# Second attention: the order of two VectorE steps, the low half of the transposed weights and the row maximum, within a half slot

## What is computed

```python
x = x + _L1_attn_ref(_layernorm(x, axis=-1), ...)

Q1, Q2 = (Q[..., :dh], Q[..., dh:])
K1, K2 = (K[..., :dh], K[..., dh:])
lam = (lam1 - lam2 + LAMBDA_INIT)[None, :, None, None]
A1 = jnp.einsum('bhqd,bhkd->bhqk', Q1, K1) * scaling
A2 = jnp.einsum('bhqd,bhkd->bhqk', Q2, K2) * scaling
attn = jax.nn.softmax(A1, axis=-1) - lam * jax.nn.softmax(A2, axis=-1)
O = jnp.einsum('bhqk,bhkd->bhqd', attn, V)
rms = jnp.sqrt(jnp.mean(O * O, axis=-1, keepdims=True) + EPS)
O = O / rms * rms_scale
O = O * (1.0 - LAMBDA_INIT)
return jnp.einsum('bne,de->bnd', O, Wo)
```

## Time and profile before

| | us |
|---|---|
| median of three runs (2936.09 to 2948.23) | 2939.1 |
| the profiled execution | 2946.47 |
| its span, first to last instruction | 2944.7 |
| PE busy in the span | 2752.8 (93%) |
| DVE busy | 2317.6 (79%) |
| ACT busy | 2126.2 (72%) |
| POOL busy | 1801.3 (61%) |

### The profile page before, as it was taken

One profiled execution on the slowest core, in us unless ns is written; L12 is line 12 of the kernel. 1 busy time (PEld: TensorE's weight loads), 2 busy tenths in 40 slices (PEclk: granted clock), 3 DMA queues, 4 the chain that ended last, 5 costly groups with the idle time before them and its releaser, 6 DMA issues.

```text
span 2944.7 us, 46590 instructions
## 1 busy us (share of the span) xinstructions
PE 2752.8 (93%) x16447; PEld 2032.8 (69%) x16447; DVE 2317.6 (79%) x4143; ACT 2126.2 (72%) x4692; POOL 1801.3 (61%) x1357
## 2 busy tenths in 40 slices
PE   6999999999899999999999999999999999999996
PEld 3333333333347777788888888888888888888885
DVE  8888888888937877789788777777777778777876
ACT  2677777777766555677877777777777787777773
POOL 3442524332015555677788777788778787777773
PEclk8899999999989999999999999999999999999997
DMA  1000000000022111000000000000000000000000
GB/s 41 7 7 7 12 7 7 7 7 2 2 76 75 48 48 58 8 1 1 1 1 3 3 1 3 3 1 3 3 1 3 3 1 3 3 1 3 3 3 6
DMA packets 25689, 34.83 MB, mean 12 GB/s; under 512 B 4136, under 2 KB 14952, under 8 KB 25456
## 3 DMA queue, kind: packets, MB, share of 16 engines
q1 hardware_dynamic: 25456, 31.85, 3.4%
HBM read 29.08 MB, written 2.23 MB: 11 GB/s over the span
## 4 chain that ended last, share of the span: by engine, by line
PE 67%; DVE 15%; ACT 8%; issue 6%; POOL 5%; DMA 0%; DVEq 0%; POOLq 0%; ACTq 0%
PE P L1798 18%; PE P L1666 9%; PE P L1825 8%; PE P L1809 6%; PE P L1651 5%; PE P L1727 5%; PE P L1639 4%; ACT a_PT L784 4%; DVE c_nm L1376 4%; DVE c_DT L1401 3%; PE P L1781 3%; PE P L1738 2%; PE P L1835 2%; PE P L1629 2%; POOL d_tn L1099 2%
## 5 line engine op out<-in xcount | busy, mean ns | idle before, releaser
L1376 DVE TENSOR_REDUCE c_nm<-P 128x1 f32<-128x1024 f32 x512 | 624.4, 1220 | 303.9 <-PE P L1798 301.9
L908 ACT ACTIVATE c_P<-P,c_nm 128x1024 f32<-128x1024 f32 x512 | 573.0, 1119 | 251.8 <-DVE c_nm L1376 247.5
L1221 DVE TENSOR_REDUCE a_mx<-P 128x1 f32<-128x512 f32 x1024 | 640.2, 683 | 99.5 <-PE P L1639 95.4
L784 ACT ACTIVATE a_PT<-P 128x512 f32<-128x512 f32 x1024 | 537.1, 603 | 165.4 <-PE P L1651 165.2
L2048 POOL TENSOR_TENSOR c_P<-c_P,c_P 128x1024 f32<-128x1024 f32 (+1 forms) x256 | 623.0, 2434 | 21.3
L2046 POOL TENSOR_SCALAR c_P<-c_P,c_rr 128x1024 f32<-128x1024 f32 (+1 forms) x256 | 300.9, 1176 | 338.4 <-DVE c_rr L1388 338.4
L1825 PE MATMUL P<-c_DT,c_xkh 128*128 128x256 f32 x2048 | 451.7, 283 | 24.7 <-DVE c_Yl L1409 23.0
L1651 PE MATMUL P<-a_Qs,a_Ks 32*128 32x512 f32 x1024 | 344.2, 493 | 59.6 <-ACT a_PT L784 53.2
L1825 PEld LDWEIGHTS P<-c_DT,c_xkh 128*128 128x128 f32 x2048 | 350.2, 189 | 37.0 <-DVE c_Yl L1409 29.2
L1798 PE MATMUL P<-c_xth,c_Th 128*128 128x512 f32 x1024 | 365.1, 437 | 2.8 <-ACT c_P L908 2.8
L1401 DVE TENSOR_TENSOR c_DT<-P,c_DT 128x512 fp32r<-128x512 f32 x512 | 348.4, 681 | 9.0 <-ACT c_DT L919 8.8
(11 more groups left out here) (245 smaller groups left out, 5393.6 us busy)
## 6 DMA issues: line engine op xcount, KB each, us to landing
b_cwB<-cw_scratch SPq DMA_DIRECT2D x64, 256.0 KB, 5.0
c_stg<-in_cw SPq DMA_DIRECT2D x8, 640.0 KB, 4.0
a_Qs<-a_mT SPq DMA_DIRECT2D x256, 2.0 KB
b_stg<-in_moe SPq DMA_DIRECT2D x9, 384.0 KB, 3.0
out<-xres SPq DMA_DIRECT2D x15, 128.0 KB, 1.8
xres<-in_x SPq DMA_DIRECT2D x3, 512.0 KB, 7.6
xres<-in_x SPq DMA_DIRECT2D x2, 256.0 KB, 3.0
a_hTl_f<-in_wqk SPq DMA_DIRECT2D x1, 512.0 KB, 3.6
```

The lines of the kernel that those rows point to most:

```text
L784: e.activation(m.PT[j][hs % 4][:, :], bank("scores", u, hs, j), ACT.Exp, scale=SCALE).then_inc(m.S["a_exp"])
L908: e.activation(m.P1[s][n % 4][:, :], P[:, k:k + 2, :].rearrange("p c k -> p (c k)"), ACT.Exp, bias=m.nm[:, n % 4, s:s + 1], accum_out=m.sm ...
L1221: e.tensor_reduce(m.mx2[u % 2][:, t // 4, j, t % 4, half:half + 1], bank("maxima", u, t, j, half), AX, ALU.max).then_inc(m.S["a_max_dve"])
L1376: e.tensor_reduce(m.nm[:, n % 4, s:s + 1], P[:, k:k + 2, :].rearrange("p c k -> p (c k)"), AX, ALU.max, negate=True).then_inc(m.S["c_nm"])
```

## The change

The step `low` is taken from behind `score` (and behind what was left of the experts) and put right behind `turn`, ahead of `score`:

```diff
@@ -473,13 +473,12 @@
         for s in range(2):
             if 3 <= n < NTAU + 3:
                 on_ring("turn", n - 3, s)
+                p.do("low", n - 3, s)
             if n < NTAU:
                 p.on(slots.take(), "score", n, s)
             left = next(moe_left, None)
             if left is not None:
                 experts(left)
-            if 3 <= n < NTAU + 3:
-                p.do("low", n - 3, s)
             if s == 0 and 0 < n <= NTAU:
                 p.do("combine", n - 1)
```

## The result

The changed kernel takes 3196.5 us (median of 4 runs, 3189.1 to 3207.5) against 2943.7 us of the kernel before (4 runs with the later one): 1.085 times as long, 95% interval 1.083 to 1.088. The difference of the medians is +252.8 us; the forecast was +253, at 3193.

The account below looks back on a forecast made before the run. TensorE set the pace at 3.31 us a half; after the change a ring through VectorE and ScalarE would: 1803 + 85 + 5 + 31 = 1924 us against 1671.5, +253, so 3193 us, range 3150 to 3250.

Parts of the forecast that it names:

- The ring's links: Second attention: exponential to copy 1.10, copy to low half 0.61, low half to maximum 0.60, maximum to exponential 1.26 us.
- the ring: Second attention: ScalarE's exponential and copy, VectorE's low half and maximum wait on each other in turn, once per half; 1803 us.
- Work in the ring: ScalarE's steps between exponential and copy: weigh 70, fourth layer's normalisation 12, layernorm's high halves 3 us; together +85 us.
- the bare ring: A half of the second attention with nothing between exponential and copy takes 3.57 us, against 3.31 before.
- Work beside the ring: ScalarE's steps between copy and exponential, +5 us, and VectorE's steps behind the maximum, +31 us, where they exceed the room.
- the term of VectorE: VectorE's steps behind the maximum, some of them the fourth layer's, exceed the room in 55 halves: +31 us.
- the third rival: TensorE's clock falls in part of the second attention, 232 us more in a fifth of the halves: 3425 us; 4%.
- the clock: TensorE in the second attention, busy for 83% at a clock near 1; costed at nothing.
- One sign: In the profile after, TensorE would wait for the exponential to free the scores' banks; its 35.3 us for low halves would go.
- The first rival: The low half fills VectorE's gap before the maximum as intended, kernel not slower: 2904 us; 3%.
- The second rival: The maximum is pushed back only where ScalarE's copy ends late, 320 copies by 165 us: about 3104 us; 4%.

Follow-up runs that it names:

- the first experiment: The changed kernel with ScalarE's weigh put behind the copy of the next half instead of ahead of it: 3126.2 us.
- the fourth experiment: Transposes and ScalarE's copy put ahead of the exponential of the half before: in the changed kernel 2896.8 us, in the kernel before 2947.9 us.
- the second experiment: The changed kernel with the low half ahead of the maximum only in halves s = 1: 2953.0 us; only in s = 0: 2998.7 us.
- experiments 5 and 6: 5: changed kernel, low half of the half before instead: 3240.3 us. 6: kernel before, low half behind combine: 2983.7; behind low half of Y too: 3131.5.

## Why the prediction was right

**The question asked first** was the right one: when does ScalarE's copy end. In 320 of 505 halves it ended after the maximum had started, and the idle 0.59 us before a maximum could not be filled without waiting for it. After, the gap is gone (1.7 us) and the time is longer, which the averages of the waits alone would not have told.

**The ring's links.** Forecast 1.10 + 0.61 + 0.60 + 1.26 = 3.57; measured 1.10 + 0.62 + 0.61 + 1.25 = 3.58 us. The links were taken where one engine really waited for the other, and so held as the whole stage came to run like this. 505 x 3.58 is 1808 us, 5 more than forecast.

**Work in the ring.** The halves with weigh take 4.16 us, as 3.57 + 0.58 said, and the first experiment took their 70 us away by moving them. The fourth layer's normalisation gives 4.34 in 15 halves (forecast 0.83 each, measured 0.76). The six halves with a high half of the layernorm take 5.5 us on the mean, 1.9 over the bare ring where I had 0.5, since VectorE has a step of its own there that waits for the high half and stands ahead of the low half. Three of the six take 4.6 us and three 6.4: in these that step takes 2.8 us in place of 0.7 (below). Together some 92 us against 85.

**Work beside the ring.** What ScalarE does between copy and exponential cost nothing that I can find: from maximum to exponential it is 1.25 us at the median, whatever stands there. I had 5 us for it. VectorE's long steps overrun in 43 of the halves with nothing else in them, by 21 us, against 31 in 55. The errors cancel: +5 and +7 for the ring and the work in it, -5 and -10 for the work beside it, so 1922.0 us were measured where 1924 were forecast. The ring is right; that the total came out within 3 us is partly luck.

**Why the term of VectorE was smaller** can be seen in the two groups that answer to the earlier trace rows:

```profile
L1484 DVE TENSOR_TENSOR d_h<-d_tn,d_sc 128x704 f32<-128x704 f32 (+1 forms) x15 | 15.2, 1010 | 0.0
...
L1474 DVE SCALAR_TENSOR_TENSOR d_tn<-d_x,d_mx 128x256 f32<-128x256 f32 x14 | 11.8, 845 | 0.0
```

The first took 1683 ns before and had 14.9 us of waits for GpSimd; the second took 1808 ns, 27.1 us in all. I took such durations as fixed, and they are not (below).

**TensorE and the rivals.** Its share of the stage is 88%, not the 83% that I forecast:

```profile
1216.00:3150.00 1934.00, 1701.55 (x10069) 1452.67 (x10070) 1286.16 (x2179) 1278.37 (x3058) 1318.85 (x892) 0.98 0.01 2
```

Its busy time has grown from 1601 to 1702 us for the same matmuls over nearly the same halves (this window is a little wider). A smaller part of that is the third rival, which did happen, weakly:

```profile
1520.00:1530.00 10.00, 7.69 (x38) 6.43 (x37) 6.73 (x11) 5.92 (x16) 6.08 (x5) 0.83 0.00 0
```

The granted clock is under 1.00 in 23 of the 193 windows of 10 us from 1220 to 3150 us, down to 0.83. These windows make about 60 us at the lower level, in which at most some 30 us of TensorE's work are lost, of the 101 us by which its busy time grew; the rest was not taken apart. The kernel before has two such windows in the stage, at 1810 and at 2560 us, also 0.83, with TensorE busy for 7.89 and 7.91 of 10 us. I had looked at the one of 1480 us alone, with 8.45 and 1.00. The rule of the Trainium skill (TensorE: Matmul & The Clock Gate, section "A second HAM failure mode: psum-queue depth-cycling"), on short idles between groups of matmuls, agrees with these traces so far that the clock goes back and forth between its levels where TensorE has short gaps. It doesn't do so at all such gaps: from 1230 to 1240 us of the trace after TensorE is busy for 6.86 us at 1.00. It cost nothing that can be seen, since TensorE no longer sets the pace: the halves with weigh last 4.16 to 4.17 us all through the stage. I had priced the clock as if TensorE were still the bound.

One sign was wrong. I had written that TensorE's waits for low halves would go and that it would wait for the exponential, which frees the scores' banks. It waits for both, and more for low halves: 136.9 us (35.3 before), against 36.9 for the exponential. The forecast doesn't rest on this, as neither is on the path: the maximum waits only 1.7 us for scores in the stage, and ScalarE's copies 1.0 us for transposes.

The first rival (the gap is filled and nothing else changes) needed a copy ahead of the exponential before it; the fourth experiment made just that and got the gain, 51 us by the pair with the copy ahead. The second rival (only late copies cost, 3104 us) fails, since the wait repeats in each half. Nor does it hold with a free half between: the 165 us of lateness are 86 in the halves s = 1 and 79 in the halves s = 0, and the second experiment measured 6 and 50. The loss through TensorE's waits, 136.9 us against 35.3, is an effect of the ring, not a cause: moving weigh alone took 70 us, while these waits fell by 15, and in the changed kernel the maximum never waits long for scores (1.7 us in all). What I had not foreseen is how near the banks are to being a bound of their own, as experiments 5 and 6 show. It did not matter for this change, which makes low halves earlier in VectorE's list and not later.

## What to carry to other kernels

An idle gap ahead of a step can be filled only by work whose input is already there. Before moving a step ahead of another, write down what it waits for, what then stands behind that wait, and whether this leads back to the step's own input; if it does, the sum of that ring's links, start to start, is the new pace wherever it is longer than the present one, and it can be read from the trace of before at the few places where each engine really waited for the next.

Where a move fails because its input is late, move the input: here both moves together gain 1.7%, where the one alone loses 8.5% and the other nothing.

## What the runs showed of the hardware

VectorE's time for one and the same instruction varies with what GpSimd does beside it. The product of 704 columns takes 1683 ns on the mean before and 1010 after, the 128 x 256 step of the earlier trace rows 1808 and 845. The low half of the layernorm goes the other way:

```profile
L1367 DVE TENSOR_TENSOR c_xkl<-xn,c_xkh 128x512 fp32r<-128x512 f32 x6 | 10.5, 1758 | 8.6 <-ACT c_xkh L883 8.6
```

It took 824 ns before. The mean of 1758 hides two kinds. Two of the six, with GpSimd's second pass over the weights (L2047) between them:

```profile
2214.62 0.69 DVE L1367 TENSOR_TENSOR c_xkl<-xn,c_xkh 128x512 fp32r<-128x512 f32 x1 [1.46 <-ACT c_xkh L883]
...
2219.16 2.38 POOL L2047 TENSOR_TENSOR c_P<-c_P,c_P 128x1024 f32<-128x1024 f32 x1
2219.27 2.82 DVE L1367 TENSOR_TENSOR c_xkl<-xn,c_xkh 128x512 fp32r<-128x512 f32 x1 [1.42 <-ACT c_xkh L883]
```

Three of the six run while GpSimd is idle and take 0.69 us. The other three start 0.10 to 0.11 us into that pass, take 2.82 to 2.83 us and end 0.55 to 0.56 us after it. The 128 x 256 step shows the same in both kernels: in the 15 cases of the stage before and the 14 after it starts while this pass runs and ends 0.28 to 0.29 us after the pass does, however long the pass still has to run. It starts 0.6 to 1.6 us into the pass before and takes 1.06 to 2.04 us; it starts 1.8 us into it after and takes 0.83 to 0.88 us. So these steps of VectorE last until GpSimd's pass is over. The profile's spans on GpSimd are rough, yet these distances repeat within 0.01 us. No experiment moved GpSimd's pass alone, so this is read from the order of times and was not tested by a change.

The maximum and the low half, which read PSUM, stay within 1215 to 1220 and 680 to 691 ns between the kernels before and after. The steps named above that vary read and write SBUF alone.
